# One block for router and tile loop, and dummy transposes on TensorE, in the last expert stage

## The chip, the cores and the metric

The kernel runs on one core of a Trainium2 chip. The metric is the device time of one execution in microseconds (us), as the median of repeated runs. Beside it stands one profiled execution, whose span and own time differ a little from that median.

The engines are called PE (TensorE), DVE (VectorE), ACT (ScalarE), POOL (GpSimd) and SP (SyncE). SP, ACT and POOL issue DMA transfers here. They run side by side and order themselves by semaphores (`wait_ge`, `then_inc`).

## The reference, cut to what matters

Four layers follow each other: attention, a feed-forward layer of experts with fixed capacity, attention again, and a second layer of experts. Only the last one is touched by the change. It takes 1024 tokens of width 256, sends each to 2 of 8 experts, and adds the weighted results:

```python
x = hidden_states                                   # layer norm of the running x, 2 x 512 tokens x 256
confidences = sigmoid(einsum('bsh,eh->bse', x, conf_w) + conf_b)
bids = confidences * wealth
top_bids, selected_experts = top_k(bids, 2)
routing_weights = softmax(top_bids)
def ffn(gw, uw, dw):                                # inner width 1024
    g = einsum('bsh,ih->bsi', x, gw)
    u = einsum('bsh,ih->bsi', x, uw)
    return einsum('bsi,hi->bsh', silu(g) * u, dw)
output = sum over the two experts of weight * ffn(expert)
```

## The kernel before, in words

The last stage is the function `moe_top2`. It has two parts, each a block of its own in which every engine has its own instruction stream. At the end of a block all engines meet, and the first part's semaphores are cleared.

**First part, norm and router.** `NormSteps` (L676 to L738) normalises the 8 groups of 128 tokens: DVE makes `pr.y` (L707), PE turns it with transposes (L723), ACT copies the result to `pr.yT` (L736). Between the transposes PE makes the logits (L1654), eight columns each. ACT writes `pr.y` to the scratch tensor `y_scr` in HBM, from which tokens are gathered later. A chain of small DVE instructions, each waiting for the one before (`link`), then finds the two best experts of each token as one-hot masks (`best`, L1697). From the mask of both (`chosen`, L1717) PE makes, with a triangular and an all-ones matrix, each token's rank inside its group and the groups' totals (L1662, L1663). DVE adds up the totals by doubling steps (L1732, L1733), counts for each expert how many tiles of 128 rows it needs (`parts`), adds those up by doubling steps too (L1748, L1749), and arrives at a slot for each token and choice (`slot_f`), then at its tile (`full`, by comparing with 22 thresholds, L1758 to L1761) and its row in the tile (`spot`, L1762). One-hot tables of tile and row (`hot_step`, `hot_token`, `hot_row`, L1766 to L1773), one round per choice, are multiplied by PE (L1668), which gives for each tile and row the token number (`rows`) and the place of its result (`dest`). `table` holds each tile's expert.

**Second part, the tile loop.** There are 23 tiles (`TILES`), enough for any split of the 2048 rows over 8 experts. For each tile T, POOL gathers 128 token rows from `y_scr` by an indirect DMA (`fetch`, L1840), PE turns them (`turn_x`, L1865), makes gate and up products in quarters (`up`, L1871) and the down products (`down`, L1881). ACT applies silu, DVE multiplies, copies the result out, and POOL scatters it to `row_scr` (`deliver`, L1848). SP loads the expert's three weight matrices, 1 MB each, into one of four buffers (`NS`): for tile 0 (always expert 0) in the first part, for T from 1 on in the second part, in order, after reading the expert's number from `table`:

```python
for T in range(1, TILES):
    e = sp.value_load(table[0:1, T:T + 1], min_val=0, max_val=E1 - 1)
    if T >= NS:
        sp.wait_ge(y_ready, T - NS + 1)
    load_weights(sp, e, T % NS)
```

PE's `begin(T)` waits for all three matrices of tile T. PE's order is: turn x and begin tile 0; then for each T the other three quarters, `turn_x(T + 1)`, `down(T, 0)`, `begin(T + 1)` (which has the first quarter of the next tile's gate products), `down(T, 1)`. At the end the results come back from `row_scr` and are added to x with the weights `share`.

Of the kernel before, what the change touches and what calls it, by code (L numbers as in the profile page):

```python
# [5 lines left out]
F32 = mybir.dt.float32  # L6
BF16 = mybir.dt.bfloat16
# [3 lines left out]
ALU = mybir.AluOpType  # L11
# [3 lines left out]
P = 128  # L15
# [14 lines left out]
EPS = 1e-5  # L30

# [1534 lines left out]
def moe_top2(pr):  # L1566
# [4 lines left out]
    with pr.stage() as c:  # L1571
# [14 lines left out]
        with pr.stage() as c1:  # L1586
            norm = NormSteps(pr, c1, "fn1")
            cw = pr.sb(c1, "conf_w", [P, DT, E1], F32)
            cb = pr.sb(c1, "conf_b", [P, E1], F32)
            wealth = pr.sb(c1, "wealth", [P, E1], F32)  # L1590
            g3 = lambda name: pr.sb(c1, name, [P, NT, E1], F32)
            g2 = lambda name: pr.sb(c1, name, [P, NT], F32)
            g1 = lambda name: pr.sb(c1, name, [P, E1], F32)
            bids, tmp, chosen, rank, rest = g3("bids"), g3("bid_tmp"), g3("chosen"), g3("rank"), g3("bid_rest")
            both = lambda name: pr.sb(c1, name, [P, 2, NT, E1], F32)
            one, pick = both("one_hot"), both("pick")
            top, low = [g2("bid0"), g2("bid1")], g2("bid_low")
            k2 = lambda name: pr.sb(c1, name, [P, 2, NT], F32)
            full, slot_f, spot = (k2(x) for x in ("full_steps", "slot_f", "spot_in"))
            total, run = g3("tile_total"), [g3("run0"), g3("run1")]  # L1600
            parts, start = g1("parts"), g1("start")
            ends = [g1("end0"), g1("end1"), g1("end2")]
            high, low_t = g2("token_high"), g2("token_low")
            part_line = pr.sb(c1, "part_line", [P, TOK // P], F32)
            step_line = pr.sb(c1, "step_line", [P, TILES], F32)
            fills = pr.sb(c1, "fills", [P, E1, TOK // P], F32)
            past = pr.sb(c1, "past", [P, TILES, 7], F32)
            over = pr.sb(c1, "over", [P, 2, NT, TILES - 1], F32)
            line = pr.sb(c1, "line", [P, P], F32)
            expert = pr.sb(c1, "expert_of", [P, TILES], F32)  # L1610
            token_f = pr.sb(c1, "token_f", [P, 2, TILES], F32)
            hot_row = pr.sb(c1, "hot_row", [P, 2 * NT, P], BF16)

            hot_step = pr.sb(c1, "hot_step", [P, 2 * NT, TILES], F32)
            hot_token = pr.sb(c1, "hot_token", [P, 2 * NT, 3, TILES], BF16)
            tps = pr.banks(c1, "gtr_ps", 2)
            rps = pr.banks(c1, "bid_ps", 3)
            ips = pr.banks(c1, "row_ps", 1)
            c_in, y_out, iota_done, l_ready, z_done, sig_done = (
                pr.sem(x) for x in ("c_in", "y_out", "iota_done", "bl_ready", "z_done", "sig_done"))  # L1620
            b_step, run_done, c_done, r_ready, diff_done, exp_done, hot_done, i_ready = (
                pr.sem(x) for x in ("b_step", "run_done", "c_done", "r_ready", "diff_done", "bexp_done", "hot_done", "i_ready"))

            with nc.Block() as block:

                @block.sync
                def _(sp):
                    sp.dma_start(cw[:], t["confT"].rearrange("(t p) e -> p t e", p=P)).then_inc(c_in, 16)
                    sp.dma_start(cb[:], t["conf_b"].partition_broadcast(P)).then_inc(c_in, 16)
                    sp.dma_start(wealth[:], t["wealth"].partition_broadcast(P)).then_inc(c_in, 16)  # L1630
                    load_weights(sp, 0, 0)
                    sp.wait_ge(y_out, 16)

                @block.gpsimd
                def _(pool):
                    g = nc.gpsimd
                    loose = dict(allow_small_or_imprecise_dtypes=True)
                    g.iota(part_line[:], pattern=[[P, TOK // P]], base=0, channel_multiplier=0,
                           **loose).then_inc(iota_done, 1)
                    g.iota(step_line[:], pattern=[[P, TILES]], base=0, channel_multiplier=0,  # L1640
                           **loose).then_inc(iota_done, 1)
                    g.iota(line[:], pattern=[[1, P]], base=0, channel_multiplier=0, **loose).then_inc(iota_done, 1)
                    g.iota(high[:], pattern=[[1, NT]], base=0, channel_multiplier=0, **loose).then_inc(iota_done, 1)
                    g.iota(low_t[:], pattern=[[0, NT]], base=0, channel_multiplier=1, **loose).then_inc(iota_done, 1)
                    norm.pool(pool)

                @block.tensor
                def _(pe):
                    def logits(j):
                        pe.wait_ge(c_in, 48)  # L1650
                        pe.wait_ge(norm.s_yT, j + 1)
                        for g in (2 * j, 2 * j + 1):
                            for k in range(DT):
                                mm = pe.matmul(rps[:, 0, g * E1:(g + 1) * E1], pr.yT[:, k, g * P:(g + 1) * P], cw[:, k],  # L1654
                                               start=(k == 0), stop=(k == DT - 1))
                        mm.then_inc(l_ready, 1)

                    norm.tensor(pe, tps, logits)
                    pe.wait_ge(c_done, 1)
                    flat = chosen[:].rearrange("p g e -> p (g e)")  # L1660

                    pe.matmul(rps[:, 1, 0:NT * E1], pr.lower[:], flat, start=True, stop=True)  # L1662
                    pe.matmul(rps[:, 2, 0:NT * E1], pr.ones[:], flat, start=True, stop=True).then_inc(r_ready, 1)  # L1663

                    for n in range(2 * NT):
                        if n % NT == 0:
                            pe.wait_ge(hot_done, 4 * (n // NT + 1))
                        mm = pe.matmul(ips[:, 0, 0:3 * TILES], hot_row[:, n],  # L1668
                                       hot_token[:, n].rearrange("p o t -> p (o t)"),
                                       start=(n == 0), stop=(n == 2 * NT - 1))  # L1670
                    mm.then_inc(i_ready, 1)

                @block.scalar
                def _(act):
                    norm.scalar(act, tps)
                    act.wait_ge(norm.s_y, NT)
                    act.dma_start(t["y_scr"].rearrange("(t p) d -> p t d", p=P), pr.y[:]).then_inc(y_out, 16)
                    act.wait_ge(z_done, 1)
                    nc.scalar.activation(bids[:], bids[:], ACT.Sigmoid).then_inc(sig_done, 1)
                    act.wait_ge(diff_done, 1)  # L1680
                    nc.scalar.activation(low[:], low[:], ACT.Exp).then_inc(exp_done, 1)

                @block.vector
                def _(dve):
                    v = nc.vector
                    n_links = [0]

                    def link(ins):

                        n_links[0] += 1  # L1690
                        ins.then_inc(b_step, 1)
                        dve.wait_ge(b_step, n_links[0])

                    wide = lambda a: a.unsqueeze(2).broadcast_to([P, NT, E1])
                    by_e = lambda a: a.unsqueeze(1).broadcast_to([P, NT, E1])

                    def best(src, value, one_hot):  # L1697

                        link(v.tensor_reduce(value[:], src[:], AX.X, ALU.max))
                        link(v.tensor_tensor(tmp[:], src[:], wide(value[:]), ALU.is_equal))  # L1700
                        link(v.tensor_tensor(tmp[:], tmp[:], by_e(pr.desc[:]), ALU.mult))
                        link(v.tensor_reduce(low[:], tmp[:], AX.X, ALU.max))
                        link(v.tensor_tensor(one_hot, by_e(pr.desc[:]), wide(low[:]), ALU.is_equal))

                    norm.vector(dve)
                    dve.wait_ge(l_ready, NT // 2)
                    v.tensor_tensor(bids[:], rps[:, 0, 0:NT * E1].rearrange("p (g e) -> p g e", g=NT), by_e(cb[:]),
                                    ALU.add).then_inc(z_done, 1)
                    dve.wait_ge(sig_done, 1)
                    link(v.tensor_tensor(bids[:], bids[:], by_e(wealth[:]), ALU.mult))  # L1710
# [324 lines left out]
```

## Time and profile before

| | |
|---|---|
| median of 3 runs | 1285.08 us (1284.66 to 1288.72) |
| the profiled execution's own time | 1284.8 us |
| its span | 1283.1 us |
| busy share of PE / DVE / ACT / POOL | 89% / 43% / 35% / 16% |
| mean granted clock of PE | 0.942 |

The span runs from the first to the last instruction that the profiler recorded; all times of day below are microseconds from its start. Busy shares are means over stages with different limits. The stage that is changed begins at about 970 us and lasts to the end.
### The profile page before, as it was taken

The numbers are of one execution on the slowest core, as the hardware profiler recorded it, in microseconds if no ns is written. First come the engines' busy times: TensorE is split into PE (matmuls) and PEld (weight loads), VectorE is DVE, ScalarE is ACT, GpSimd is POOL, SyncE is SP. The second block draws the span as 40 slices with busy tenths as digits, with TensorE's granted clock in tenths as the row PEclk, the third lists the DMA queues.
The fourth block names the chain that finished last, engine by engine and source line by source line (L and its number), as shares of the span: only waits on it lengthen the run. The fifth ranks groups of instructions, "written<-read, shape, count | busy, mean of one in ns | idle before, by whom it ended". The sixth has DMA issues, their size and how long they took to land. (4 is left out here: it accounts for less than half of the span.)

```text
span 1283.1 us, 19035 instructions
## 1 busy us (share of the span) xinstructions
PE 1141.3 (89%) x7144; PEld 722.2 (56%) x7144; DVE 558.1 (43%) x1586; ACT 445.2 (35%) x584; POOL 204.7 (16%) x334
## 2 busy tenths in 40 slices
PE   5878999999959999999848999999985599999993
PEld 2432333333447888888625333333334499999993
DVE  5565777774363111111256776666315211111112
ACT  4355666666412111111033455555642011110110
POOL 4461322224100000000013000000200111111110
PEclk9998999999959999999878999999996699999997
DMA  8528222200273333445059122230003698988843
GB/s 222 147 100 176 38 38 38 38 1 1 99 263 50 132 131 131 161 177 163 22 211 186 17 38 38 38 38 2 1 1 133 252 374 307 322 319 316 310 144 107
DMA packets 95876, 169.43 MB, mean 132 GB/s; under 512 B 8529, under 2 KB 65569, under 8 KB 94770
## 3 DMA queue, kind: packets, MB, share of 16 engines
q1 hardware_dynamic: 89570, 157.59, 41.6%
q0 software_dynamic: 2208, 6.03, 1.6%
q10 hardware_dynamic: 4016, 4.72, 1.1%
q8 instruction: 51, 0.84, 0.3%
q14 instruction: 31, 0.25, 0.1%
HBM read 148.34 MB, written 19.79 MB: 131 GB/s over the span
## 5 line engine op out<-in xcount | busy, mean ns | idle before, releaser
L1126 ACT ACTIVATE prob<-st_ps 128x1024 f32<-128x1024 f32 x256 | 253.9, 1022 | 187.6 <-PE st_ps L1024 105.3
L217 DVE CUSTOM_DVE_ANT_0 junk<-s_ps,bias_rows,mx 128x512 f32<-128x512 f32 x236 | 168.0, 748 | 67.1 <-PE s_ps L202 66.3
L1016 PE MATMUL st_ps<-q_stack,k_stack 100*128 100x512 bf16 x512 | 185.5, 386 | 9.4 <-ACTq L1105 6.6
L202 PE MATMUL s_ps<-k_stack,q_stack 97*128 97x512 bf16 x468 | 178.1, 391 | 10.9 <-DMA q_stack<-q_scr 6.6
L217 DVE CUSTOM_DVE_ANT_0 junk<-s_ps,bias_rows 128x512 f32<-128x512 f32 x232 | 153.3, 689 | 75.2 <-PE s_ps L202 74.6
L1512 PE MATMUL h_ps<-expert_in,w 128*128 (+1 forms) x704 | 155.0, 382 | 2.3 <-PEq L65 2.3
L1512 PEld LDWEIGHTS h_ps<-expert_in,w 128*128 128x128 f32 (+1 forms) x704 | 132.7, 189 | 23.1 <-issue 2.5
L1036 PE MATMUL o_ps<-prob,v_unit 128*32 128x512 f32 x1024 | 139.9, 600 | 1.0 <-ACT prob L1126 1.0
L202 PEld LDWEIGHTS s_ps<-k_stack,q_stack 97*128 97x128 bf16 x468 | 45.5, 99 | 145.8 <-DVE mx L217 82.4
L1915 ACT ACTIVATE silu<-gu_ps 128x512 f32<-128x512 f32 x46 | 27.5, 597 | 225.8 <-PE gu_ps L1871 221.1
L1021 PE MATMUL st_ps<-bias_hi,ident_bf 128*128 128x512 bf16 x256 | 98.1, 383 | 0.0
L1542 ACT ACTIVATE gelu_out<-h_ps 128x256 f32<-128x256 f32 (+1 forms) x88 | 33.7, 383 | 182.2 <-PE h_ps L1512 182.2
L1016 PEld LDWEIGHTS st_ps<-q_stack,k_stack 100*128 100x128 bf16 x512 | 48.8, 99 | 82.6 <-ACT prob L1126 37.0
L1871 PE MATMUL gu_ps<-xg_T,wg 128*128 128x128 f32 x736 | 91.3, 278 | 0.6 <-DVE xg_T L1924 0.6
L1871 PEld LDWEIGHTS gu_ps<-xg_T,wg 128*128 128x128 f32 x736 | 89.2, 195 | 2.1 <-issue 1.0
L1871 PE MATMUL gu_ps<-xg_T,wu 128*128 128x128 f32 x736 | 89.6, 275 | 0.0
L1553 DVE TENSOR_TENSOR hid<-gelu_out,h_ps 128x256 f32<-128x256 f32 (+1 forms) x88 | 37.0, 421 | 118.2 <-ACT gelu_out L1542 118.2
L1871 PEld LDWEIGHTS gu_ps<-xg_T,wu 128*128 128x128 f32 x736 | 87.6, 192 | 1.1
L1881 PE MATMUL y_ps<-wd,silu_up 128*128 128x256 f32 x368 | 86.9, 379 | 0.0
L1521 PE MATMUL e_ps<-w,hid 128*128 128x256 f32 (+1 forms) x352 | 77.3, 379 | 0.0
L1930 DVE TENSOR_TENSOR silu_up<-silu,gu_ps 128x512 f32<-128x512 f32 x46 | 31.6, 687 | 103.9 <-PE gu_ps L1871 103.9
L1521 PEld LDWEIGHTS e_ps<-w,hid 128*128 128x128 f32 (+1 forms) x352 | 66.9, 190 | 9.4
(271 smaller groups left out, 1129.6 us busy)
## 6 DMA issues: line engine op xcount, KB each, us to landing
wg<-in_gateT SPq DMA_DIRECT2D x23, 1024.0 KB
wu<-in_upT SPq DMA_DIRECT2D x23, 1024.0 KB
wd<-in_downT SPq DMA_DIRECT2D x23, 1024.0 KB
w<-in_w SPq DMA_DIRECT2D x16, 1368.0 KB
k_stack<-k_scr SPq DMA_DIRECT2D x96, 128.0 KB, 5.2
w<-in_w SPq DMA_DIRECT2D x8, 1280.0 KB
k_scr<-k_parts SPq DMA_DIRECT2D x24, 256.0 KB, 2.4
q_stack<-q_scr SPq DMA_DIRECT2D x96, 64.0 KB, 5.6
```

The lines of the kernel that those rows point to most:

```text
L202: pe.matmul(self.ps[:, self.bank("job", u, j)], stack(self.pr.Q[b], MROW, i % 2, h, slice(qt * P, (qt + 1) * P)), stack(self.pr.K[b], MROW ...
L217: self.pr.nc.vector.tensor_tensor_reduce(out=self.junk[:, self.bank("job", u, j)], in0=self.ps[:, self.bank("job", u, j)], in1=self.m.bias ...
L1016: pe.matmul(st_ps[:, h], stack(K[b], ROWS, i % 2, h, slice(kt * P, (kt + 1) * P)), stack(Q[b], ROWS, i % 2, h, slice(0, SQ)), start=True, ...
L1021: mm = pe.matmul(st_ps[:, h], pr.ident_bf[:], m.bias_hi[:, kt], start=False, stop=True)
L1036: mm = pe.matmul(o_ps[32 * h:32 * h + 32, 0], V[u % B][:, kt, h], prob[:, kt % 2, h], start=(kt == 0), stop=(kt == KT - 1))
L1126: nc.scalar.activation(prob[:, kt % 2, 2 * hp:2 * hp + 2], st_ps[:, 2 * hp:2 * hp + 2], ACT.Exp).then_inc(exp_done, 1)
L1512: mm = pe.matmul(h_ps[0:hn, j % 4, off:off + 256], w[:, k, h0:h0 + hn], ein[:, k, bass.ds(e, 1)], start=(k == 0), stop=(k == DT - 1))
L1521: mm = pe.matmul(e_ps[:, s, r * 256:(r + 1) * 256], hid[0:hn, j, r * P:(r + 1) * P], w2[s][0:hn, j], start=(j == 0), stop=(j == NJ - 1))
L1542: nc.scalar.activation(act_out[0:hn, j % 4], h_ps[0:hn, j % 4, 0:256], ACT.Gelu_apprx_tanh).then_inc(gelu_done, 1)
L1553: nc.vector.tensor_tensor(hid[0:hn, j], act_out[0:hn, j % 4], h_ps[0:hn, j % 4, 256:512], ALU.mult).then_inc(hid_done, 1)
L1871: mm = pe.matmul(gu_ps[:, bank, j * P:(j + 1) * P], w[:, T % NS, k, (4 * h + j) * P:(4 * h + j + 1) * P], xgT[:, T % 2, k], start=(k == 0) ...
L1881: mm = pe.matmul(y_ps[:, 0, 0:D], prod[:, h, j * P:(j + 1) * P], wd[:, T % NS, 4 * h + j], start=(h == 0 and j == 0), stop=(h == 1 and j = ...
```

## The change

The two parts become one block, with one instruction stream for each engine, so that nothing is cleared and nobody meets between router and tile loop. PSUM banks are shared between the two (`tps`, `lps`, `rps`, `ips` lie in the loop's banks). In detail:

- SP reads the table only after `table_done`, and waits for the first two gathers (`xg_in[0]`, `xg_in[1]`) before it issues tile 1's weights.
- Ranks and totals come from nine bf16 products that accumulate in one PSUM bank: the triangular matrix once, and the ones matrix for each distance between groups. `chosen` is bf16 and has a ninth group of zeros, whose product holds the totals. Both doubling chains are gone; the tiles that lie ahead of an expert come from a product with a fixed mask (`sooner`) and one reduction.
- The tile of a slot comes from scaling and rounding (`ROUND`) in two instructions in place of the compare with 22 thresholds.
- The one-hot tables are made by three engines: DVE makes `hot_step` for both choices, the first eight rows of `hot_row` and `hot_token` 0; ACT makes `hot_token` 1 and 2; POOL makes the last eight rows one by one, and PE waits for each.
- `rows` comes ahead of `dest`, and POOL waits for `rows` and `y_out` alone before it gathers; `dest` is awaited before the first delivery. The shares come last on DVE.
- PE makes 14 transposes of the identity before the norm and 20 behind the table products, into the bank `xt_ps`, whose content nobody reads.

The core of the diff (declarations and unchanged lines of the moved part left out):

```diff
+ROUND = 1.5 * 2.0 ** 23
...
             @block.sync
+                load_weights(sp, 0, 0)
+                sp.wait_ge(table_done, 1)
+                for s in range(2):
+                    sp.wait_ge(xg_in[s], 16)
                 for T in range(1, TILES):
...
             @block.gpsimd
+                norm.pool(pool)
+                g.iota(below[:], pattern=[[1, E1], [-1, E1]], base=0, channel_multiplier=0,
+                       **loose).then_inc(fill_done, 1)
+                g.memset(chosen[:, NT], 0.0).then_inc(fill_done, 1)
+                g.tensor_copy(lower_bf[:], pr.lower[:]).then_inc(fill_done, 1)
+                g.tensor_copy(ones_bf[:], pr.ones[:]).then_inc(fill_done, 1)
+                pool.wait_ge(fill_done, 1)
+                g.tensor_scalar(sooner[:], below[:], 0.0, None, ALU.is_gt).then_inc(fill_done, 1)
+                pool.wait_ge(spot_done, 1)
+                pool.wait_ge(iota_done, 4)
+                for n in range(NT):
+                    g.tensor_scalar(hot_row[:, NT + n], line[:], spot[:, 1, n:n + 1], None,
+                                    ALU.is_equal).then_inc(row_done, 1)
+                pool.wait_ge(rows_done, 1)
+                pool.wait_ge(y_out, 16)
...
                 def deliver(T):
+                    if T == 0:
+                        pool.wait_ge(dest_done, 1)
...
             @block.tensor
+                def stay_warm(n):
+                    for _ in range(n):
+                        pe.transpose(xt_ps[:, 0, 0:P], pr.ident[:], pr.ident[:])
+                stay_warm(14)
+                norm.tensor(pe, tps, logits)
+                pe.wait_ge(fill_done, 4)
+                pe.wait_ge(c_done, 1)
+                pe.matmul(rps[:, 0:(NT + 1) * E1], lower_bf[:], flat, start=True, stop=False)
+                for far in range(1, NT + 1):
+                    mm = pe.matmul(rps[:, far * E1:(NT + 1) * E1], ones_bf[:], flat[:, 0:(NT + 1 - far) * E1],
+                                   start=False, stop=(far == NT))
+                mm.then_inc(r_ready, 1)
+                pe.wait_ge(tok_done, 4)
+                for n in range(2 * NT):
+                    if n == 0:
+                        pe.wait_ge(own_row, 1)
+                    elif n >= NT:
+                        pe.wait_ge(row_done, n - NT + 1)
+                    mm = pe.matmul(ips[:, 0:3 * TILES], hot_row[:, n],
+                                   hot_token[:, n].rearrange("p o t -> p (o t)"),
+                                   start=(n == 0), stop=(n == 2 * NT - 1))
+                mm.then_inc(i_ready, 1)
+                stay_warm(20)
...
             @block.scalar
+                act.wait_ge(step_done, 1)
+                nc.scalar.activation(hot_token[:, :, 1], hot_step[:], ACT.Copy, scale=low_t[:, 0:1]).then_inc(tok_done, 1)
+                for k in range(2):
+                    mine = slice(k * NT, (k + 1) * NT)
+                    nc.scalar.activation(hot_token[:, mine, 2], hot_step[:, mine], ACT.Copy,
+                                         scale=float(k + 1)).then_inc(tok_done, 1)
...
             @block.vector
-                    link(v.tensor_copy(total[:], flat(2)))
-                    src = total
-                    for i, step in enumerate((1, 2, 4)):
-                        dst = run[i % 2]
-                        v.tensor_copy(dst[:, 0:step], src[:, 0:step]).then_inc(run_done, 1)
-                        v.tensor_tensor(dst[:, step:], src[:, step:], src[:, 0:NT - step], ALU.add).then_inc(run_done, 1)
...
+                link(v.tensor_tensor(fills[:], count.unsqueeze(2).broadcast_to([P, E1, TOK // P]),
+                                     part_line[:].unsqueeze(1).broadcast_to([P, E1, TOK // P]), ALU.is_gt))
+                link(v.tensor_reduce(parts[:], fills[:], AX.X, ALU.add))
+                link(v.tensor_scalar(parts[:], parts[:], 1.0, None, ALU.max))
+                link(v.tensor_tensor(below[:], sooner[:], parts[:].unsqueeze(1).broadcast_to([P, E1, E1]), ALU.mult))
+                link(v.tensor_reduce(start[:], below[:], AX.X, ALU.add))
+                link(v.scalar_tensor_tensor(out=rank[:], in0=by_e(start[:]), scalar=float(P),
+                                            in1=rps[:, 0:NT * E1].rearrange("p (g e) -> p g e", g=NT),
+                                            op0=ALU.mult, op1=ALU.add))
+                link(v.tensor_tensor(pick[:], one[:], rank[:].unsqueeze(1).broadcast_to([P, 2, NT, E1]), ALU.mult))
+                link(v.tensor_reduce(slot_f[:], pick[:], AX.X, ALU.add))
+                link(v.tensor_scalar(full[:], slot_f[:], 1.0 / P, 0.5 / P - 0.5, ALU.mult, ALU.add))
+                link(v.tensor_scalar(full[:], full[:], ROUND, ROUND, ALU.add, ALU.subtract))
+                v.scalar_tensor_tensor(out=spot[:], in0=full[:], scalar=-float(P), in1=slot_f[:],
+                                       op0=ALU.mult, op1=ALU.add).then_inc(spot_done, 1)
+                v.tensor_tensor(hot_step[:], full[:].rearrange("p k g -> p (k g)").unsqueeze(2)
+                                .broadcast_to([P, 2 * NT, TILES]), ...).then_inc(step_done, 1)
+                v.tensor_tensor(hot_row[:, 0:NT], ...).then_inc(own_row, 1)
+                v.tensor_tensor(hot_token[:, :, 0] ...).then_inc(tok_done, 1)
...
+                v.tensor_copy(table[:], expert[:]).then_inc(table_done, 1)
+                dve.wait_ge(i_ready, 1)
+                link(v.tensor_copy(token_f[:], ips[:, TILES:2 * TILES]))
+                v.scalar_tensor_tensor(out=rows[:], in0=ips[:, 0:TILES], scalar=float(P),
+                                       in1=token_f[:], op0=ALU.mult, op1=ALU.add).then_inc(rows_done, 1)
```

## Rows read from the trace of the kernel before

**Rows 1.** Chain of waits: start us, us, what (last stage).
```profile
1003.76 6.48 DMA xg<-y_scr,row_token
1011.59 9.01 PE gu_ps L1871 x64
...
1022.54 1.78 PE gu_ps L1871 x16
...
1033.36 1.78 PE gu_ps L1871 x16
...
1263.61 3.13 DMA row_scr<-y_rows,row_dest
```

**Rows 2.** Timeline, PE alone: start us, us, engine, line, operation, out<-in.
```profile
954.76 1.50 PE L1169 MATMUL o_tok_ps<-ident,o_all 128*128 128x128 f32 x12 [1.49 <-PEq L65]
...
980.06 1.09 PE L723 MATMUL gtr_ps<-ident,y_tok 128*128 128x128 f32 x4
...
980.95 3.42 PE L1654 MATMUL bid_ps<-conf_w,y_T 128*128 128x8 f32 x16
```

**Rows 3.** Timeline of the router.
```profile
988.53 0.23 DVE L1717 TENSOR_TENSOR chosen<-one_hot 128x64 f32<-128x64 f32 x1
...
990.04 0.22 DVE L1727 COPY tile_total<-bid_ps 128x64 f32<-128x64 f32 x1 [0.32 <-PE bid_ps L1663]
...
994.39 0.52 DVE L1758 TENSOR_TENSOR over<-slot_f,step_line 128x352 f32<-128x352 f32 x1
...
995.51 0.17 DVE L1762 SCALAR_TENSOR_TENSOR spot_in<-full_steps,slot_f 128x16 f32<-128x16 f32 x1
...
996.79 1.22 DVE L1773 TENSOR_TENSOR hot_row<-spot_in,line 128x1024 bf16<-128x1024 f32 x1
...
1000.27 0.65 PE L1668 MATMUL row_ps<-hot_token,hot_row 128*128 128x69 bf16 x8 [1.56 <-DVE hot_row L1773]
```

**Rows 4.** Stretches: busy us (count) of PE, PEld, DVE, ACT, POOL; clock, DMA, GB/s.
```profile
1006.00:1008.00 2.00, 0.00 (x0) 0.00 (x0) 0.00 (x0) 0.00 (x0) 0.38 (x1) 0.50 1.01 399
...
1014.00:1016.00 2.00, 2.00 (x16) 2.00 (x15) 0.00 (x0) 0.60 (x1) 0.00 (x0) 0.75 1.07 391
```

**Rows 5.** Stretches, PE alone: length, busy us (count), granted clock, DMA, GB/s.
```profile
380.15:383.57 3.42, 1.78 (x4) 0.50 0.12 31
...
653.22:656.63 3.41, 3.41 (x12) 0.51 0.98 404
...
953.59:957.01 3.42, 2.11 (x18) 1.00 0.02 5
...
967.25:970.66 3.41, 1.20 (x6) 0.99 0.00 0
...
974.07:977.49 3.42, 3.42 (x16) 0.50 0.99 375
```

**Rows 6.** Groups of POOL by shape: count, busy us, mean ns.
```profile
L440 POOL TENSOR_TENSOR k_parts<-kq_rest,k_parts 128x512 bf16<-128x512 f32 x16 | 18.5, 1159 | 8.3 <-ACT k_parts L575 8.3
...
L258 POOL TENSOR_SCALAR mneg<-mx 128x8 f32<-128x8 f32 x32 | 8.0, 249 | 212.3 <-DVE mx L217 210.9
...
L440 POOL TENSOR_TENSOR q_parts<-kq_rest,q_parts 128x512 bf16<-128x512 f32 x4 | 5.9, 1470 | 0.9 <-ACT q_parts L575 0.9
...
L431 POOL TENSOR_SCALAR wq<-wq 128x512 f32<-128x512 f32 x1 | 1.5, 1499 | 0.0
...
L89 POOL CAST ident_bf<-ident 128x128 bf16<-128x128 f32 x1 | 0.3, 291 | 0.1
```

**Rows 7.** The gathers' tile xg: time from issue to landing.
```profile
DMA to landing us min/median/max: 3.7/6.3/7.2
```

**Rows 8.** Timeline of SP's issues for tiles 1 and 2.
```profile
1003.92 0.39 SPq L1582 DMA_DIRECT2D wg<-in_gateT  x1
...
1004.92 0.42 SPq L1584 DMA_DIRECT2D wd<-in_downT  x1
...
1006.11 2.80 SPq L1582 DMA_DIRECT2D wg<-in_gateT  x1
```

More of the change, by code:

```diff
@@ new lines, in moe_top2 @@
+        norm = NormSteps(pr, c, "fn1")
+        cw = pr.sb(c, "conf_w", [P, DT, E1], F32)
+        cb = pr.sb(c, "conf_b", [P, E1], F32)
+        wealth = pr.sb(c, "wealth", [P, E1], F32)
+        g3 = lambda name: pr.sb(c, name, [P, NT, E1], F32)
+        g2 = lambda name: pr.sb(c, name, [P, NT], F32)
+        g1 = lambda name: pr.sb(c, name, [P, E1], F32)
+        bids, tmp, rank, rest = g3("bids"), g3("bid_tmp"), g3("rank"), g3("bid_rest")
+        chosen = pr.sb(c, "chosen", [P, NT + 1, E1], BF16)
@@ new lines, in moe_top2 @@
+        lower_bf = pr.sb(c, "lower_bf", [P, P], BF16)
+        ones_bf = pr.sb(c, "ones_bf", [P, P], BF16)
+        below = pr.sb(c, "below", [P, E1, E1], F32)
+        sooner = pr.sb(c, "sooner", [P, E1, E1], F32)
+        both = lambda name: pr.sb(c, name, [P, 2, NT, E1], F32)
+        one, pick = both("one_hot"), both("pick")
+        top, low = [g2("bid0"), g2("bid1")], g2("bid_low")
+        k2 = lambda name: pr.sb(c, name, [P, 2, NT], F32)
+        full, slot_f, spot = (k2(x) for x in ("full_steps", "slot_f", "spot_in"))
@@ new lines, in moe_top2 @@
+        parts, start, end = g1("parts"), g1("start"), g1("end")
+        high, low_t = g2("token_high"), g2("token_low")
+        part_line = pr.sb(c, "part_line", [P, TOK // P], F32)
+        fills = pr.sb(c, "fills", [P, E1, TOK // P], F32)
+        past = pr.sb(c, "past", [P, TILES, 7], F32)
+        line = pr.sb(c, "line", [P, P], F32)
+        expert = pr.sb(c, "expert_of", [P, TILES], F32)
+        token_f = pr.sb(c, "token_f", [P, TILES], F32)
+        hot_row = pr.sb(c, "hot_row", [P, 2 * NT, P], BF16)
@@ new lines, in _ @@
+                norm.vector(dve)
+                dve.wait_ge(l_ready, NT // 2)
+                v.tensor_tensor(bids[:], lps[:, 0:NT * E1].rearrange("p (g e) -> p g e", g=NT), by_e(cb[:]),
+                                ALU.add).then_inc(z_done, 1)
+                dve.wait_ge(sig_done, 1)
+                link(v.tensor_tensor(bids[:], bids[:], by_e(wealth[:]), ALU.mult))
+                best(bids, top[0], one[:, 0])
+                link(v.tensor_scalar(tmp[:], one[:, 0], -1.0, 1.0, ALU.mult, ALU.add))
@@ new lines, in _ @@
+                link(v.tensor_tensor(rest[:], bids[:], tmp[:], ALU.mult))
+                link(v.scalar_tensor_tensor(out=rest[:], in0=one[:, 0], scalar=-BIG, in1=rest[:],
+                                            op0=ALU.mult, op1=ALU.add))
+                best(rest, top[1], one[:, 1])
+                dve.wait_ge(fill_done, 5)
+                v.tensor_tensor(chosen[:, 0:NT], one[:, 0], one[:, 1], ALU.add).then_inc(c_done, 1)
+                v.tensor_tensor(low[:], top[1][:], top[0][:], ALU.subtract).then_inc(diff_done, 1)
@@ L1922, in turn_x_out @@
+                dve.wait_ge(exp_done, 1)
+                link(v.tensor_scalar(top[0][:], low[:], 1.0, None, ALU.add))
+                link(v.reciprocal(share[0][:], top[0][:]))
+                link(v.tensor_tensor(share[1][:], low[:], share[0][:], ALU.mult))
                 def turn_x_out(T):
```

247 lines of the change are left out of this document (74 added, 173 removed).

## The prediction

> **What bounds the kernel now.** The chain of waits is read first, from the end [rows 1]. From 1011.59 us on it is TensorE (PE) almost without a break: tile 1 starts its gate products at 1022.54, tile 2 at 1033.36, so one tile costs 10.82 us, and the 22 tiles behind the first follow at that pace. The change touches nothing inside a tile. What it can move is the time at which tile 1 begins; the whole rest of the stage then moves with it, as long as each tile's weights are there. So I count the shift of that one point, 1022.54.
>
> Ahead of it lie three stretches, read from the timeline and the stretches [rows 2, 3, 5]: the norm and logits, bound by PE (974.0 to 984.37, no gap in the stretches); the router, a chain of small VectorE (DVE) instructions behind them; and the way from there to tile 1, with the gather's 6.48 us [rows 1]. The granted clock is 0.5 from about 970.7 until 1015 [rows 4, 5], that is 1.2 GHz where the tile loop has 2.4.
>
> **Norm and logits: 14 dummy transposes.** Cold, four transposes take about 0.92 us of PE (0.23 each, from the pieces around 980.06) and sixteen logit instructions 3.42 (0.214 each) [rows 2]. 16 of the first and 32 of the second make 3.7 + 6.8 = 10.5, which is the stretch. Warm, a transpose costs 0.125 (12 in 1.50) [rows 2]; a logit instruction is not seen warm, so half of 0.214. Laid out with the ScalarE (ACT) copies of 0.60 between them, the last logit would then come at about 980.0 instead of 984.4: a gain of 4.3 us is the upper bound, nothing the lower one, since 14 dummies cold take 14 x 0.23 = 3.2 us and end at 973.9, just when PE's first transposes of normalised tokens start now (974.0).
> Do transposes lift the clock? The stretch from 653.22 to 656.63 held 2.1 us of transposes of y_tok and then 1.3 us of query products, and the clock was up at its end; the stretch from 380.15, with 1.78 us of dense dispatch products alone, left it at 0.50. And 953.59 to 957.01, with transposes only, kept 1.00, where 1.20 us of work and then silence, from 967.25, lost it [rows 5]. So here transposes do count. The Trainium skill says the contrary ("TensorE: Matmul & The Clock Gate", Part 4: PE-mode transpose: the full clock does not engage for them, since they don't count as work in the same way); by that page this term would be nothing, and the rows just named speak against it.
> But the logits that follow are eight columns wide, and the same mix never raised the clock between 974 and 984 (granted 0.50 throughout) [rows 5]. It may fall again halfway. I take 2.5 us, between 1.8 (lost a third of the way) and 4.3 (kept), a little nearer to the low end.
>
> **Router up to the slots.** The chosen mask is ready at 988.53 + 0.23 = 988.76, the copy of the totals starts at 990.04, and the slots are known at 995.51 + 0.17 = 995.68 [rows 3]. That is 6.92 us. Between copy and slots lie 25 instructions, among them the two prefix sums of six instructions each, and the compare with 22 thresholds and its reduction (0.52 each). The new form has nine bf16 products in place of four f32 instructions (0.65 for eight bf16 ones of like shape [rows 3], so 0.75, plus 0.2 of hand-over) and eleven DVE instructions, five of 64 elements at about 0.26 from start to start, two of 128 at 0.32 and four of 8 or 16 at 0.20: 2.7 us in all. The mean of the old 25 (5.64 / 25 = 0.23) would give 2.5. New 3.6, gain 3.3 (3.0 to 3.6). The share ratios, formerly between, go behind the destinations, where DVE has nothing to do until the gather lands. The bf16 fills on GpSimd (POOL) come right behind its part of the norm, where it has nothing else to do until the slots are known.
>
> **From the slots to the first gather.** Before: 1003.76 - 995.68 = 8.08 us, made of two rounds of one-hot tables on DVE (each hot_row 1.22), the products (the second eight at 1000.27 for 0.65), four small instructions of about 0.2 and, for what is left until 1003.76, near 2 us, the change of block [rows 1, 3]. Now three engines share the tables. DVE: hot_step of 368 elements (0.54, by the 352 of over at 0.52), half the rows (1.22), one token table: ready 2.2 us behind the slots. ACT: three copies, about 0.4 each, ready before that. POOL: eight one-hot rows, 128 elements each, which the trace does not show. Nearest are its TENSOR_SCALAR of 512 elements at 1.50 and of 8 at 0.25, which give 0.25 + 120 x 2.5 ns = 0.54, and its CAST of 128 elements at 0.29 [rows 6]. I take the former, it is the same operation: 8 x 0.52 = 4.1. One and the same subtraction took POOL 1.16 us in one group and 1.47 in another [rows 6]; for such a stretch beside a busy DVE I add 0.3. The products of the second half come one by one behind the rows, so the last adds only 0.15. Then copy, row numbers (0.4) and hand-over 0.2. Sum 5.2 us, gain 2.9. With rows at 0.29, DVE's tables bound instead: 2.3 + 1.3 (16 products, 0.65 for eight) + 0.6 = 4.2, gain 3.9; with rows 1.5 times dearer 7.2, gain 0.9.
> The Trainium skill has GpSimd share its SBUF interfaces with VectorE and contend with instructions that have two SBUF inputs ("GPSIMD Engine Reference", 8. Key points); hot_row on DVE is such a one. By that page the rows would be slowed for as long as hot_row lasts; no row here prices it by itself.
> The block's end disappears (its barrier and clearing), but all that ran in SP and POOL before it is now in one queue with the loop: behind POOL's rows stand its gathers, which need them anyway; the output wait on y_scr is long past, its transfer began before the router did.
>
> **From the first gather to tile 1.** Before, 1022.54 - 1003.76 = 18.78 us: gather 6.48, 1.35 for turning x, products with a cold part [rows 1]. Loads and gathers were issued together; DMA runs full from 1006 [rows 4]. Gathers take 3.7 us at best, 6.3 in the middle [rows 7]; and a delivery of rows issued into a quiet queue at 1263.61 took 3.13 [rows 1]. So gather 0 lands at 3.6, gather 1, issued 1.6 later, at about 5.2. Now SP waits for both, then reads the table (0.77 between the end of tile 1's last issue, 1004.92 + 0.42, and tile 2's first at 1006.11) and issues [rows 8]. Flow was full 2.1 us behind the issue at 1003.92, and 3.15 MB at 391 to 399 GB/s need 8.0 [rows 4, 8]. Tile 1's weights are thus there at 5.2 + 0.15 + 0.77 + 2.1 + 8.0 + 0.2 = 16.4. PE alone would want them at 3.6 + 1.35 + 10.95 - 1.7 (no cold part) = 14.2, so a new wait of 2.2 us stands ahead of begin(1), with down(0,1) and through y_ready tile 4's load behind it; both have slack. Gain 18.78 - 16.4 = 2.4; bounds 1.4 (gathers a microsecond slower) and 4.6 (weights not the bound). The second batch of dummies, 20 x 0.23 = 4.6 us cold, ends about when gather 0 lands; it can delay turning x by half a microsecond, which the wait for the weights hides. It would cost it outright if the weights came first. A warm first tile is worth nothing for the same reason.
> Tile 2's weights follow 8.2 us behind tile 1's, PE wants them 10.82 later; no second wait.
>
> **Sum.** 2.5 + 3.3 + 2.9 + 2.4 = 11.1 us. The profiled execution has 1284.8 us (span 1283.1), 0.3 under the median of 1285.08. So 1284.8 - 11.1 = 1273.7, and 1274.0 beside the median.
>
> **Rivals.**
> 1. The dummies do not lift the clock in the norm: PE's 10.5 us stay. For it: the mix of transposes and logits ran cold for 10 us of unbroken PE work [rows 5]; against it the three stretches named above. Gain 8.6, 1276.5 us. The page on the clock gate would have it this way.
> 2. POOL's compare is dear, 0.8 us or more: the last product waits. For it: nothing shows this operation; against: 512 elements take 1.5. Gain 8.8, 1276.3.
> 3. The gathers take 6.5 us in a quiet queue too, the weights start 3 us later, tile 1 begins at 19.3: a loss of 0.5 there. Against: the 3.7 and the 3.13. Gain 8.2, 1276.9.
> 4. The new wait of 2.2 us ahead of tile 1 drops the clock, as the silence of about 2.2 us before 970.66 did [rows 5]; a cold part like tile 0's, 1011.6 to 1015, costs 1.7. Gain 9.4, 1275.7.
> 5. Slower than before: the place is POOL's eight rows. They must first eat 11.1 us, so each would have to cost 0.52 + 11.1 / 8 = 1.9 us, and 2.4 us for a loss above 0.3%: 1289.0. A row of 128 elements would then cost more than 512 do [rows 6].
>
> **How the numbers follow.** A measurement of this kernel tells about 0.3%, 3.9 us, from no change. Chances: the forecast 0.48, rival 1 0.20, rival 2 0.11, rival 3 0.08, rival 4 0.07, rival 5 0.04, half of it within 3.9 us of before; 0.02 is left for several terms at their poor ends, which end within 3.9 us too. The fast end is all terms nearly at their best, 4.0 + 3.5 + 3.9 + 3.6 = 15.0, 1270.0. The slow end, rivals 1 and 2 or 1 and 3 together, is a gain near 6, 1279.0. So faster 0.94, same 0.04, slower 0.02.
>
> **What would show it.** Right: granted clock 1.0 for part of 974 to 982 and the last logit before 983; about 3.6 us from the mask to the slots; POOL's rows near 0.5 us each and ending after DVE's tables; the first gather landing in 4 us; an idle PE of about 2 us ahead of tile 1, charged to the load of its weights; tile period 10.82. Wrong: a logit stretch of 10 us, or rows on POOL near 1 us, or PE waiting again ahead of tile 2 or 3.

## The result

The changed kernel takes 1275.82 us in the median of its first four runs (1273.90 to 1277.19), against 1285.24 for the one before: a ratio of 0.992, with a 95% interval of 0.990 to 0.994. It was run five more times later (the run `again` below, ratio 0.995, 0.9937 to 0.9963); the median of all nine is 1277.2. So the gain is 9.4 us in the first four and 7.7 in the later five (against 1285.83 for the kernel before there). Forecast were 1274.0, between 1270 and 1279.

Single times of one kernel spread by up to 8 us, and a good part of that comes from ahead of the change: in 13 profiled executions, two of the changed kernel and one of each other, the last stage began, with SP's first issue, anywhere from 969.3 to 975.0 us. So the steps are compared by intervals from that issue (970.62 before, 972.10 after). Up to the bids they hardly vary: in the ten traces with the dummies ahead of the norm the bids come 9.48 to 9.52 us behind it.

The norm of the changed kernel in the timeline (start us, us, engine, line, operation, operands), against [rows 2]:

```profile
972.14 3.19 PE L1744 MATMUL xt_ps<-ident 128*128 128x128 f32 x14 [2.22 <-PEq L66]
...
975.52 1.30 PE L724 MATMUL gu_ps<-ident,y_tok 128*128 128x128 f32 x8 [0.18 <-DVE y_tok L708]
...
979.61 1.97 PE L1737 MATMUL gu_ps<-conf_w,y_T 128*128 128x8 f32 x16
...
981.62 0.22 DVE L1867 TENSOR_TENSOR bids<-gu_ps,conf_b 128x64 f32<-128x64 f32 x1 [4.22 <-PE gu_ps L1737]
```

Sixteen logit instructions take 1.97 us where they took 3.42. The clock in stretches, PE alone, against [rows 5]:

```profile
972.19:975.60 3.41, 3.23 (x15) 0.50 0.33 35
975.60:979.02 3.42, 3.27 (x27) 1.00 0.98 380
979.02:982.43 3.41, 2.56 (x23) 1.00 1.04 385
...
1009.74:1013.15 3.41, 1.02 (x6) 1.00 1.10 373
1013.15:1016.56 3.41, 3.41 (x16) 0.50 1.02 401
```

It rises at 975.6, behind nothing but transposes, and stays up until the last logit is done. Further down is a loss: PE stands still from 1010.7 to 1013.06, and the clock is at 0.50 for the 3.4 us behind that. The tables, against [rows 3]:

```profile
985.74 0.22 DVE L1878 TENSOR_TENSOR chosen<-one_hot 128x64 bf16<-128x64 f32 x1
...
989.17 0.17 DVE L1899 SCALAR_TENSOR_TENSOR spot_in<-full_steps,slot_f 128x16 f32<-128x16 f32 x1
...
989.45 5.96 POOL L1700 TENSOR_SCALAR hot_row<-line,spot_in 128x128 bf16<-128x128 f32 x8 [15.25 <-DVE spot_in L1899]
989.71 1.22 DVE L1906 TENSOR_TENSOR hot_row<-spot_in,line 128x1024 bf16<-128x1024 f32 x1
...
995.47 0.24 PE L1764 MATMUL y_ps<-hot_token,hot_row 128*128 128x69 bf16 x1 [0.34 <-POOL hot_row L1700]
...
995.97 0.18 DVE L1920 SCALAR_TENSOR_TENSOR row_token<-y_ps,token_f 128x23 uint32<-128x23 f32 x1
...
997.07 1.29 POOL L1708 DMA_INDIRECT xg<-y_scr,row_token  x1 [1.65 <-DVE row_token L1920]
```

POOL's eight rows are the end of that path: PE's last product waits for them, and everything up to the gather waits for the product. From the gather on, the chain of waits, against [rows 1]:

```profile
998.66 2.79 DMA xg<-y_scr,row_token
...
1003.53 9.49 DMA wd<-in_downT
1013.06 3.68 PE gu_ps L1779 x16
...
1025.78 1.78 PE gu_ps L1779 x16
```

A gather lands in 2.8 us, and a new link stands in the chain, the load of tile 1's last matrix. Tile 2 begins 12.72 us behind tile 1, where a tile costs 10.82 elsewhere.

One thing about these starts: where PE runs from one tile into the next without a wait, the chain puts the start 0.16 to 0.17 us behind the first product of the timeline (tile 2 of the changed kernel: 1025.78 in the chain, 1025.61 in the timeline); behind a wait the two are the same (1013.06). The prediction counted by the chain, and so does the table. By the timeline 12.72 is 12.55, and a tile behind a wait that kept the clock takes 10.92 where the chain has 11.08 or 11.09.

All intervals in us from the stage's first issue; "end" is the end of the span. The first gather is taken at its issue, the tiles at their first gate product in the chain of waits.

| kernel | bids | slots known | first gather | tile 1 | tile 2 | end | median us |
|---|---|---|---|---|---|---|---|
| before | 13.78 | 25.06 | 33.14 | 51.92 | 62.74 | 312.5 | 1285.2 to 1285.8 |
| changed | 9.52 | 17.24 | 24.97 | 40.96 | 53.68 | 303.4 | 1275.8 |
| again | 9.51 | 17.25 | 24.96 | 41.19 | 53.77 | 303.5 | 1278.2 |
| no_first | 13.82 | 21.55 | 29.29 | 45.55 | 56.63 | 306.3 | 1278.8 |
| no_second | 9.51 | 17.24 | 24.96 | 41.19 | 52.28 | 301.9 | 1276.1 |
| rows_dve | 9.51 | 17.26 | 22.96 | 40.24 | 52.97 | 303.2 | 1273.4 |
| wait_one | 9.51 | 17.24 | 24.96 | 39.20 | 50.29 | 299.9 | 1273.3 |
| early_load | 9.51 | 17.26 | 24.99 | 44.55 | 55.37 | 305.1 | 1277.1 |
| wait_warm | 9.50 | 17.24 | 24.98 | 42.42 | 53.51 | 303.3 | 1275.7 |
| before_dummies | 9.48 | 20.76 | 28.85 | 48.04 | 58.86 | 308.6 | 1280.9 |
| best_dve | 9.51 | 17.24 | 22.77 | 37.98 | 48.80 | 298.7 | 1270.3 |
| rows_pool | 9.51 | 17.24 | 28.57 | 45.69 | 59.43 | 309.2 | 1281.2 |
| before_wait | 13.77 | 25.04 | 33.13 | 49.38 | 60.46 | 310.2 | 1283.0 |

### The profile page after: what moved, and what is told of

Same layout as the page of the kernel before. It is cut to its first block and busy times, and to the rows that moved or that the text cites. A ratio compares the mean times of both kernels' runs of the same rounds, so it can differ in the third digit from the quotient of the medians.

```text
span 1275.5 us, 19065 instructions
## 1 busy us (share of the span) xinstructions
PE 1142.1 (90%) x7159; PEld 723.1 (57%) x7183; DVE 553.3 (43%) x1566; ACT 446.6 (35%) x587; POOL 212.0 (17%) x346
## 5 line engine op out<-in xcount | busy, mean ns | idle before, releaser
L1022 PE MATMUL st_ps<-bias_hi,ident_bf 128*128 128x512 bf16 x232 | 88.8, 383 | 0.0
```

What stands on the lines that cost most here:

```text
L1022: mm = pe.matmul(st_ps[:, h], pr.ident_bf[:], m.bias_hi[:, kt], start=False, stop=True)
```

## The experiments

**again.** The changed kernel, nothing edited.

> The changed kernel once more, for its spread. Its first four runs lay in two pairs, 1277.1 to 1277.2 and 1273.9 to 1274.6. Theory: the profiled run lost the clock for 3.4 us at the head of tile 1, after PE had waited 2.4 us for the weights, which cost 1.9 us there; whether that happens differs from run to run, so the times fall into the same two heaps, some 2 to 3 us apart, median between 1274 and 1277. Rival: the two pairs are drift of the stages ahead of the change (they were 1.5 us later in this profiled execution than in that of before); then tile 1 to tile 2 takes 12.7 us in every execution, and the spread comes from ahead of 972 us.

The five times were 1276.3, 1277.7, 1278.2, 1279.0 and 1282.0: no two heaps. The profiled one lost the clock at tile 1 as the first had (12.58 us from tile 1 to tile 2). The intervals repeat within 0.25 us, and the two traces differ more in where the stage begins (1.0 us), where the rival put the spread. The other seven executions, that of 1282.0 among them, have no trace, so where their times differ is not shown. But the lost clock at tile 1 is no drift, it is in both traces.

**no_first** and **before_dummies**, the same part taken away and put in alone:

```diff
-                stay_warm(14)
```

> The changed kernel without the 14 dummy transposes ahead of the norm. Theory: they alone made the clock rise in the norm, so without them the clock is 0.5 there and norm and logits take 13.8 us from the first issue of the stage to the bids instead of 9.5: 4.3 us slower than the changed kernel, about 1280 us. Rival (a page of the Trainium skill, that transposes do not lift the clock): the rise at 975.6 was luck of the moment, the real transposes would have had it too, and nothing changes, 1275.8 us.

```diff
+                    for _ in range(14):
+                        pe.transpose(ips[:, 0, D:D + P], pr.ident[:], pr.ident[:])
                     norm.tensor(pe, tps, logits)
```

> The kernel before with one part of the change alone, the 14 dummy transposes ahead of the norm. Theory: norm and logits take 9.5 instead of 13.8 us here too, nothing else moves: 4.3 us faster than before, 1281.2 against 1285.5. Rival: the gain in the changed kernel needed the single block; then 13.8 us stay and the time is that of before.

```profile
983.85 0.22 DVE L1866 TENSOR_TENSOR bids<-gu_ps,conf_b 128x64 f32<-128x64 f32 x1 [8.51 <-PE gu_ps L1737]
```

That is the first kernel, whose stage began at 970.03; the second, whose stage began at 974.16, has

```profile
983.64 0.23 DVE L1709 TENSOR_TENSOR bids<-bid_ps,conf_b 128x64 f32<-128x64 f32 x1 [4.21 <-PE bid_ps L1654]
```

Without the dummies 13.82 us, with them alone 9.48: they are worth 4.3 us at the bids, in either kernel. At the end of before_dummies 3.8 us of them are left (308.6 against 312.5), since tile 0's cold part got 0.4 us longer. By the medians the second is 4.5 us faster than before (1280.87 against 1285.41, ratio 0.9962, interval 0.9949 to 0.9975). The rule of the Trainium skill ("TensorE: Matmul & The Clock Gate", Part 4: PE-mode transpose), that the full clock does not engage for transposes, does not hold here: the full clock came behind fourteen transposes of the identity, and did not come without them.
At the end of no_first only 2.9 us of the 4.3 are left, since there the clock survived a wait of 2.64 us ahead of tile 1 (11.08 us to tile 2). So such a wait does not lose it every time. For the same reason the medians show little here: no_first has 1278.8, the changed kernel 1278.2 in the executions beside it and 1275.8 in the first four. The 4.3 us rest on the intervals and on before_dummies.

**no_second.**

```diff
-                stay_warm(20)
```

> The changed kernel without the 20 dummy transposes behind the table products. Theory: tile 0 starts cold and takes 1.7 us longer, all of it inside the 2.4 us that PE waits for tile 1's weights anyway; the shorter wait no longer drops the clock in tile 1, so the kernel is as fast or up to 1.9 us faster: 1274 to 1276 us. Rival: the second dummies are needed, tile 1 begins later without them: 1.7 us slower, 1277.5 us.

Tile 1 begins at 41.19, as in again, and PE waits 0.20 us for its weights instead of 2.60; tile 2 follows 11.09 us later instead of 12.58, as the theory had it (median 1276.1, 1274 to 1276 expected). The second batch of dummies buys nothing here and goes with a loss of 1.5 us: a faster first tile only means a longer standstill ahead of the second.

**rows_dve**: POOL's loop over rows is dropped, and

```diff
+                v.tensor_tensor(hot_row[:, NT:], spot[:, 1].unsqueeze(2).broadcast_to([P, NT, P]),
+                                line[:].unsqueeze(1).broadcast_to([P, NT, P]), ALU.is_equal).then_inc(row_done, 1)
```

> The changed kernel with all sixteen one-hot rows on DVE, POOL's eight rows gone. Theory: POOL's rows are the end of the path from slots to gather (5.96 us, the first one 1.88 while DVE made its own rows, the others 0.60 each). On DVE the last row and the token table are ready 3.4 us behind the slots, sixteen products take 1.3, so the first gather goes out 1.7 us earlier than in the changed kernel (slots to gather 6.0 instead of 7.7 us): 1274.1 us. Rival: DVE, now with the expert table behind 1.1 us more of rows, becomes the end and eats the gain: within 0.5 us of the changed kernel.

The gather goes out 2.0 us earlier (22.96), a little more than the theory said; ACT still makes its part of the token tables. Tile 1 gains only 0.7 to 0.95 of it: from the last issue of its weights to its begin it took 10.75 us, where the changed kernel and again took 9.5 and 9.7, and the clock fell all the same (12.73 us to tile 2). Why that load was slower is not settled. The median is 1273.4 (1274.1 expected), 3.8 us below the changed kernel's nine, while the end of the stage in this trace is only 0.2 us earlier: the profiled execution took 1276.1, three of the other five 1271.7 to 1272.5. No trace shows what those did otherwise.

Tile 0 lost the clock too: it was up from 995.10 to 998.51, raised by the second batch of dummies, then at 0.50 until 1001.92. Ahead of that fall PE stood for 1.06 us until the gather landed, made two transposes, and stood for 0.68 more. In the changed kernel, with 0.39 and 0.68, it was kept.

**rows_pool**: POOL makes all sixteen rows, DVE none.

> The changed kernel with all sixteen one-hot rows on POOL and none on DVE, to price a row of POOL. Theory: POOL stood still during its first row because DVE was making its rows at the time (1.88 us against 0.60 for the others); with those rows gone from DVE the first row costs about 0.6 to 1.2 (hot_step and the token table of DVE still run beside it), so sixteen rows take 9.6 to 10.3 us. Rival: the first instruction of POOL there is dear for a reason of its own (a start behind a long wait); then the first row costs 1.9 again and the sixteen take 10.9. Either way 4 us slower than the changed kernel, about 1281.

The tile's instructions on POOL (ns min/median/max), first in the changed kernel, then in this one:

```profile
L1700 POOL TENSOR_SCALAR hot_row<-line,spot_in x8: 598/604/1882, 989.5 to 994.8; 128x128 bf16<-128x128 f32 x8
```

```profile
L1700 POOL TENSOR_SCALAR hot_row<-line,spot_in x16: 601/605/831, 989.7 to 998.6; 128x128 bf16<-128x128 f32 x16
```

The sixteen rows take 9.56 us by the timeline (9.6 to 10.3 expected), the first gather goes out 3.6 us later, and the median is 1281.2, as expected. The dear first row is gone with DVE's rows: it takes 0.83 us instead of 1.88, behind a wait of POOL as long as before (15.2 us), so the rival is out. DVE's hot_row thus costs POOL 1.05 us; the 0.23 left over the 0.60 of the others are beside hot_step and DVE's hot_token (0.53 and 0.59 us), which still run then. The Trainium skill ("GPSIMD Engine Reference", 8. Key points) has POOL contend with VectorE instructions of two SBUF inputs. All three are such instructions, and the trace agrees.

**before_wait**, the wait alone in the kernel before:

```diff
+                for s in range(2):
+                    sp.wait_ge(xg_in[s], 16)
                 for T in range(1, TILES):
```

> The kernel before with one part of the change alone: SP waits for the first two gathers ahead of tile 1's weights. Theory: gather 0 lands 2.9 us behind its issue instead of 6.5, and tile 1, now bound by its weights, begins 16.0 to 16.5 us behind the first gather's issue instead of 18.8; its wait for them is short, since tile 0 starts cold and needs PE for 11 us: 2.3 to 2.8 us faster, 1283 against 1285.5. Rival: the load, 5.5 us later, costs as much as the earlier gather gives: no change.

Tile 1 begins 2.54 us earlier, 16.25 behind the gather, and the stage ends 2.3 us earlier; by the medians 2.8 us (1282.95 against 1285.79; ratio 0.9982, interval 0.9971 to 0.9993). **early_load** takes the same wait out of the changed kernel:

> The changed kernel without the wait for the gathers: SP issues tile 1's weights as soon as the expert table is there, about 5 us ahead of the first gather. Theory: the gathers run beside the loads and land 6 us or more behind their issue instead of 2.8, so tile 0 begins 3.5 us later; but tile 1's weights are there long before it ends, so PE never waits and keeps its clock: tile 1 begins 4.2 us (turn and first products) + 9.3 behind that, 17.5 us behind the first gather's issue instead of 16.0, and tile 2 10.82 behind it instead of 12.7: within 1.5 us of the changed kernel either way, 1276 to 1278. Rival (what the change seems to be made for): the wait is worth the gathers' whole delay, and without it the kernel is 3.5 us slower than the changed one, 1280.5.

Its gathers, against [rows 7]:

```profile
DMA to landing us min/median/max: 5.5/6.7/6.7
```

Tile 1 begins 3.4 to 3.6 us later than in the changed kernel, two more than expected, because PE stood still for 4 us ahead of the gather and made tile 0's first sixteen products in 3.75 us instead of 2.02. But then it waits for nothing, and tile 2 is only 1.6 to 1.7 us behind. The medians cannot tell the two apart (1277.1 and 1277.2). So the wait is worth something, but half of it is given back at tile 1.

**wait_one**: wait for less, and read the table ahead of the wait.

```diff
-                for s in range(2):
-                    sp.wait_ge(xg_in[s], 16)
                 for T in range(1, TILES):
                     e = sp.value_load(table[0:1, T:T + 1], min_val=0, max_val=E1 - 1)
+                    if T == 1:
+                        sp.wait_ge(xg_in[0], 16)
```

> The changed kernel, in which SP reads tile 1's expert first and then waits for the first gather alone before it issues tile 1's weights. Theory: the first flow of a load comes 2 us behind its issue, so an issue at the landing of gather 0 (2.8 us behind its own issue) collides with neither gather; tile 1's weights are there 2.5 us earlier, 13.5 instead of 16.0 us behind the first gather's issue, which is before PE wants them (14.0). No wait ahead of tile 1, no lost clock: tile 1 begins 2 us earlier and tile 2 10.8 to 11.1 us behind it, together 2 to 4 us faster than the changed kernel, whose nine runs have a median of 1277.2: 1274. Rival: the second gather is caught by the load, lands 6 us behind its issue instead of 3, and tile 1 waits for it, not for the weights: it has slack until 11 us behind the first gather's issue, so it would have to take over 9 us to show.

```profile
1001.39 9.92 DMA wd<-in_downT
1011.36 2.05 PE gu_ps L1779 x16
...
1022.45 1.78 PE gu_ps L1779 x16
```

The weights are issued 3.26 us behind the first gather instead of 5.46, both gathers still land within 3.1, so the rival is out, PE waits 0.67 us, and the clock stays. Tile 2 begins 3.4 us earlier than in the changed kernel; the median is 1273.3. The run changes two things at once, but the traces part them: in the changed kernel gather 1 lands 4.38 us behind the first issue and the weights go out 1.08 later, here gather 0 lands at 3.08 and they go out 0.18 later. So 1.3 us come from waiting for one gather less and 0.9 from reading the table ahead.

**wait_warm**: dummies in the standstill.

```diff
                     down(T, 0)
+                    if T == 0:
+                        pe.wait_ge(xT_done, 2)
+                        for _ in range(18):
+                            pe.transpose(xt_ps[:, 0, D:D + P], pr.ident[:], pr.ident[:])
```

> The changed kernel with 18 dummy transposes between down(0,0) and the wait for tile 1's weights, 2.25 us at full clock, so that PE does not stand still there. Theory: the clock is then kept in every execution, tile 1 takes 10.8 to 11.1 us instead of 12.7; 1.7 us faster than the changed kernel where that one lost the clock: 1275.5 against its 1277.2, and the slow heap of times is gone. Rival: a stillness of 2.4 us doesn't lose the clock by itself, the change of level came from the mix of work; then 12.7 us stay.

```profile
1008.26 2.13 PE L1817 MATMUL xt_ps<-ident 128*128 128x128 f32 x18
...
1012.31 2.05 PE L1779 MATMUL gu_ps<-xg_T,wg 128*128 128x128 f32 x16 [1.93 <-DMA wd<-in_downT]
```

The clock was kept, 11.09 us to tile 2. But the weights took 10.9 us from their last issue, nearly as in rows_dve, so that the end is no better than in the changed kernel (303.3), though the median is (1275.7 against 1277.2). The dummies filled only part of the wait: 1.93 us of standstill were left behind them. That a wait filled in part keeps the clock agrees with the theory; since no_first kept it unfilled, one trace does not prove it.

**best_dve**: wait_one, and on DVE the token table first, then both halves of the rows.

> The changed kernel with both repairs: all one-hot rows on DVE, now behind the token table, so that the first eight products run while the last eight rows are made; and SP waiting for gather 0 alone, with tile 1's expert read ahead of the wait. Theory: the repairs stand on different stretches and add up. Slots to first gather: 0.5 + 0.5 + 1.1 + 1.1 for the tables, 0.7 for the last eight products, 0.8 to the issue, and one wait behind the expert table (about 1 us of DVE behind the rows): 5.3 to 5.7 us, against 7.7 in the changed kernel and 5.9 with the rows on DVE and the token table last. First gather to tile 1: 14.2 us as in the run that waited for one gather. Stage from its first issue to the end: 299.9 - 2.2 = 297.7 us; time 1271 us. Rival: the first gather, 2 us earlier, finds PE's 20 dummies in its way, so that the first tile begins no earlier; then 299.5 and 1273.

```profile
986.40 0.17 DVE L1894 SCALAR_TENSOR_TENSOR spot_in<-full_steps,slot_f 128x16 f32<-128x16 f32 x1
...
988.66 1.22 DVE L1908 TENSOR_TENSOR hot_row<-spot_in,line 128x1024 bf16<-128x1024 f32 x1
...
989.93 0.65 PE L1759 MATMUL y_ps<-hot_token,hot_row 128*128 128x69 bf16 x8 [0.42 <-DVE hot_row L1908]
...
992.10 1.29 POOL L1703 DMA_INDIRECT xg<-y_scr,row_token  x1 [20.66 <-DVE row_token L1917]
```

1270.26 us (1269.73 to 1270.78), ratio 0.9881 (0.9867 to 0.9895): faster than both kernels. From slots to gather 5.5 us instead of 7.7, and no wait ahead of tile 1. The stage takes 298.7 us, 1.0 more than expected, since tile 0 ran cold at its head (its first sixteen products took 3.50 us), with little slack left to hide that in. The dummies were not in the way, they ended 1.1 us before the gather landed. But the clock that they raised was lost again, as in rows_dve (stretches, PE alone):

```profile
989.82:993.23 3.41, 3.30 (x22) 0.50 0.00 0
993.23:996.64 3.41, 1.64 (x12) 1.00 0.53 96
996.64:1000.05 3.41, 3.41 (x18) 0.50 0.80 317
```

PE stood for 1.10 us until the gather landed and for 0.68 us behind its two transposes, and 0.3 us into tile 0 the clock fell. So this kernel lost its 3.4 us of full clock at tile 0, where the changed kernel lost it at tile 1.

## Why the prediction was right, step by step

The time lay in the range, 1.8 us above the forecast (3.2 by the median of all nine), and the forecast case did come true in its mechanism, with one term much too large and rival 4 on top of it. In the profiled executions 11.1 us were forecast and 9.1 came (312.5 less 303.4). Part of that closeness is luck: one term came out 2.5 us short and a loss of 1.9 us was not in the sum, while the other three terms gave 2.4 us more than forecast.

- **Norm and logits, 2.5 forecast:** 4.26 measured (13.78 less 9.52), the upper bound. The caution was about a clock that falls again among the narrow logits; it held until the last one. no_first and before_dummies show that the dummies did it. Rival 1 is out.
- **Router up to the slots, 3.3:** 3.56 (25.06 - 13.78 less 17.24 - 9.52). The eleven instructions go from 986.62 to 989.34, the 2.7 us of the sum. No run has this part alone; the gain is read from the two traces, where the router is what changed in this stretch (before_dummies, with the old chain and the dummies, has the old 11.28 us, 20.76 less 9.48, against 7.72).
- **From the slots to the first gather, 2.9:** 0.35 (8.08 less 7.73). This is the term of the sum that was mis-sized, by 2.5 us. POOL's eight rows took 5.96 instead of 4.4: 0.60 each instead of 0.52, and 1.3 us for the start beside DVE's tables, for which 0.3 had been added. (The prediction's own estimate from the rows was 0.54; it then reckoned with 0.52, which is worth 0.2 us.) And from the row numbers on DVE to the indirect DMA on POOL it takes 0.92 us (996.15 to 997.07), not 0.2. Rival 2 set its condition at 0.8 us a row, and a row alone cost 0.60; but with the dear first one the eight took 0.75 each in the mean, PE's last product waited for them, and the loss of 2.5 us is close to the 2.3 that rival 2 had priced. So this term went rival 2's way. Splitting the tables over three engines did not shorten them: from the slots to the end of the last product it was 5.24 us before (995.68 to 1000.92) and 6.37 after (989.34 to 995.71). The gain of 0.35 comes from behind the products, 2.84 us before and 1.36 after, where the end of the block is gone; no run has that alone. With all rows on DVE, in the better order, the stretch is 5.5.
- **From the first gather to tile 1, 2.4:** 2.79. Gathers land in 2.8 to 3.1 us, the weights are there 16.0 behind the first gather, against 16.4 in the sum, and PE waits 2.4 us, against 2.2. before_wait has nearly the same gain by itself, 2.53 (18.78 less 16.25 from the gather to tile 1). Rival 3 is out, and so is rival 5, which needed rows of 1.9 us. (By the timeline this term is 2.63 and the next one 1.73; the sum is the same.)
- **Tile 1 to tile 2, taken as unchanged:** 12.72 instead of 10.82, a loss of 1.9 us. This is rival 4, at its price of 1.7. It came in the changed kernel's two traces and in rows_dve and rows_pool; no_first escaped it with a wait as long. That it is the standstill and not the mix of work is borne out by wait_one, no_second and before_wait, which wait 0.20 to 0.81 us for tile 1's weights, and by best_dve, which does not wait for them: they keep the clock there. How long a standstill has to be is not settled: at tile 0 rows_dve and best_dve lost the clock behind shorter ones, in two pieces. The prediction saw the wait coming at its length, and gave this loss a chance of 0.07.

Check: 4.26 + 3.56 + 0.35 + 2.79 - 1.9 = 9.1.

## What to carry to other kernels

When a step is split over engines, price the slowest share beside what the others do at the same time; here it was 2 us faster to leave POOL out of it. A transfer that is held back to protect a small one should be issued when its first bytes will come right behind the small one's last, not when the small one has landed: half of what the wait gave at tile 1 was gone at tile 2, because it was two microseconds too long; of these, 0.9 were a table read that could be done ahead. And speeding up work ahead of a fixed arrival only lengthens the wait, which can cost the clock too.

## What the hardware showed that was not expected

- Behind fourteen f32 transposes of the identity (3.19 us at the half clock) the granted clock rose from 0.50 to 1.00, and 32 logit instructions of eight columns, with 16 transposes among them, kept it; the same mix without the dummies ran at 0.50 for 10.4 us.
- A standstill of 2.1 to 2.6 us was followed by the half clock in three traces (changed, again, rows_dve), one of 3.5 in rows_pool too; one of 2.64, in no_first, was not. At tile 0, standstills of 1.1 and 0.68 us with two transposes between were followed by it in rows_dve and best_dve, while 0.90 and 0.68 in no_first were not.
- A POOL compare of 128 elements with a per-partition scalar costs 0.60 us, 0.83 beside two two-input DVE instructions of 0.53 and 0.59 us, and 1.88 when a third of 1.22 us runs beside it too.
- An indirect gather of 128 rows of 1 KB lands 2.8 to 3.3 us behind its issue when no load runs (first two gathers of before_wait and of the kernels with the wait), and 5.5 to 6.7 beside one (first three of early_load).
